# A decoder kernel on one core: the first normalisation moved ahead of the weights, and the first decay chain moved from VectorE to GpSimd

## The reference

```python
def _layernorm(x, axis=-1, eps=1e-05):
    m = jnp.mean(x, axis=axis, keepdims=True)
    v = jnp.var(x, axis=axis, keepdims=True)
    return (x - m) / jnp.sqrt(v + eps)

# _L0_attn, for the normalised x, two heads h of 128 features, chunks of 64 tokens
rk = x.reshape(Bs, Ts, H, d);  rk = rk / max(norm(rk), 1e-12)
beta = sigmoid(einsum('btd,hd->bth', x, W_beta))
log_decay = -exp(A_log) * softplus(einsum('btd,hd->bth', x, W_alpha) + dt_bias)
cum = cumsum(log_decay, -1)                       # within a chunk
L_mask = tril(exp(tril(cum[:, None] - cum[None, :])))
```

## Time and profile before

| what | value |
|---|---|
| median of 3 runs | 5632.31 us (5630.9 to 5637.03) |
| the profiled execution | 5640.22 us |
| its span, first to last instruction | 5637.7 us |
| PE, DVE, POOL, ACT busy | 4736.9, 4265.8, 3826.9, 2325.5 us |
| end of the piece in front of the loop | about 330.8 us into the span |
| mean granted TensorE clock | 0.95 |

### The profile page before, as it was taken

The page is one execution under the profiler, slowest core; times in us unless marked ns, Lnnn a source line. Parts: engine busy times, 40 slices in busy tenths (PEclk is TensorE's granted clock), DMA queues, the critical chain, the costliest instruction groups (busy, mean ns, idle before and its releaser), DMA issues.

```text
span 5637.7 us, 105981 instructions
## 1 busy us (share of the span) xinstructions
PE 4736.9 (84%) x28362; PEld 3112.3 (55%) x28362; DVE 4265.8 (76%) x11558; ACT 2325.5 (41%) x4480; POOL 3826.9 (68%) x10625
## 2 busy tenths in 40 slices
PE   1069898888889889888988988898898889889888
PEld 0045655656566465655646565565656556565655
DVE  5868777777777778777777878777787877778777
ACT  0034344444334444444444444444443444444344
POOL 1158676785867678586767858676785867768585
PEclk7589999999999999999999999999999999999999
DMA  3000000000000000000000000000000000000000
GB/s 85 8 12 1 28 1 13 16 9 20 1 24 5 11 18 9 20 1 24 5 9 20 9 20 1 24 5 9 20 5 24 1 24 5 9 20 1 20 1 16
DMA packets 61879, 78.07 MB, mean 14 GB/s; under 512 B 11168, under 2 KB 53808, under 8 KB 61232
## 3 DMA queue, kind: packets, MB, share of 16 engines
q1 hardware_dynamic: 52784, 62.42, 3.4%
q10 hardware_dynamic: 8448, 8.39, 0.4%
HBM read 45.04 MB, written 8.46 MB: 9 GB/s over the span
## 4 chain that ended last, share of the span: by engine, by line
PE 58%; DVE 23%; issue 8%; ACT 8%; POOL 1%; SPq 1%; DMA 1%; DVEq 0%; ACTq 0%; POOLq 0%
PE bank L1171 8%; PE bank L1090 6%; PE bank L1204 5%; PE bank L1076 5%; PE bank L1102 4%; PE bank L1000 3%; PE bank L1124 3%; PE bank L1007 3%; PE bank L1189 2%; PE bank L1111 2%; DVE arena L2004 2%; PE bank L1082 2%; ACT arena L763 2%; ACT arena L750 1%; PE bank L1132 1%
## 5 line engine op out<-in xcount | busy, mean ns | idle before, releaser
L746 ACT ACTIVATE arena<-bank 128x512 f32<-128x512 f32 x768 | 454.4, 592 | 386.9 <-PE bank L1090 386.9
L1775 DVE TENSOR_REDUCE smax<-bank 128x4 f32<-128x512 f32 x768 | 525.5, 684 | 114.6 <-PE bank L1082 66.1
L1779 DVE TENSOR_TENSOR arena<-bank,smax 128x512 f32<-128x512 f32 x768 | 531.2, 692 | 26.4
L1090 PE MATMUL bank<-ident,arena 128*128 128x128 f32 x3072 | 489.4, 282 | 46.9 <-ACT arena L737 29.2
L1171 PE MATMUL bank<-w,arena 128*128 128x512 f32 x1024 | 482.2, 601 | 14.0 <-DVE arena L1727 14.0
L1102 PE MATMUL bank<-arena 128*32 128x128 f32 x6144 | 329.1, 286 | 192.3 <-ACT arena L750 192.3
L1076 PE MATMUL bank<-arena 64*128 64x512 f32 x1536 | 436.4, 645 | 64.4 <-ACT arena L774 28.0
L1090 PEld LDWEIGHTS bank<-ident,arena 128*128 128x128 f32 x3072 | 348.7, 142 | 247.8 <-ACT arena L739 83.0
L1204 PE MATMUL bank<-w,arena 128*128 128x256 f32 x2048 | 454.1, 380 | 13.9 <-ACT arena L809 13.9
L737 ACT ACTIVATE arena<-arena,rstd 128x512 f32<-128x512 f32 x512 | 368.2, 719 | 203.4 <-DVE arena L1779 197.5
L1204 PEld LDWEIGHTS bank<-w,arena 128*128 128x128 f32 x2048 | 387.8, 190 | 90.3 <-issue 23.0
(11 more groups left out here) (428 smaller groups left out, 11948.0 us busy)
## 6 DMA issues: line engine op xcount, KB each, us to landing
arena<-in_x_dram SPq DMA_DIRECT2D x35, 512.0 KB, 3.5
xn_next<-arena SPq DMA_DIRECT2D x17, 512.0 KB, 2.9
arena<-cum_dram SPq DMA_DIRECT2D x17, 512.0 KB, 3.7
arena<-in_ctx_dram SPq DMA_DIRECT2D x16, 512.0 KB, 3.5
out_dram<-arena ACTq DMA_DIRECT2D x16, 512.0 KB, 3.1
xn<-xn_next SPq DMA_DIRECT2D x15, 512.0 KB, 2.9
w<-in_L_ffn_w_dram SPq DMA_DIRECT2D x8, 512.0 KB
w<-in_L_ffn_w_dram SPq DMA_DIRECT2D x1, 1024.0 KB
```

The lines of the kernel that those rows point to most:

```text
L746: act.activation(PT[:, v % 2], bank[3 + v % 2][:, :].rearrange("p (h q) -> p h q", h=QH), ACT.Copy).then_inc(S["pt"], 1)
L1090: ins = tr(bank[3 + v % 2][:, j * P:(j + 1) * P], Ssb[:, v % 4, j, :], ident[:, :])
L1775: dve.tensor_reduce(smax[:, u, :], sc, AX, ALU.max).then_inc(S["s_max"], 1)
L1779: dve.tensor_tensor(Ssb[:, u % 4], sc, smax[:, u, :].unsqueeze(2).broadcast_to([P, QH, P]), ALU.subtract).then_inc(S["s_sub"], 1)
```

## The change

The first `x_in` load and the two `W_alpha` loads are issued ahead of all other loads, and the latter get a semaphore of their own (`first_rows`). VectorE splits `W_alpha` and does the first norm before it waits for the weights; its set-up follows, then the second norm and the keys. GpSimd runs the first chain, behind its set-up and in front of `centered`. ScalarE's wait for weights and masks moves behind the first square-root seed. In the piece ahead of the loop both halves of a norm use the first set of scratch tiles.

```diff
         @block.sync
+            sp.dma_start(x_in[:, :, :], x_d[0]).then_inc(loaded_x, 16)
+            for h in range(DH):
+                sp.dma_start(dw[0][:, h, :], a["L0_attn_W_alpha"][h].partition_broadcast(P), ...).then_inc(first_rows, 16)
             for dst, src in loads:                 # without the two W_alpha loads
...
-            sp.dma_start(x_in[:, :, :], x_d[0]).then_inc(loaded_x, 16)
             sp.dma_start(xres[:, :, :], x_d[0]).then_inc(loaded_r, 16)
         @block.gpsimd
+            first = [0]
+            def first_link(operation, *operands, known=False, behind=0):
+                if first[0] > behind and not known:
+                    pool.wait_ge(first_step, first[0] - behind)
+                operation(*operands).then_inc(first_step, 1)
+                first[0] += 1
+            pool.wait_ge(set_dve, 2)
+            pool.wait_ge(moved_now, 16)
+            for j in range(SLICES):
+                chain_products(pool, first_link, xn0[:, :, :], j)
+                chain_links(pool, first_link, j, 0, 16)
+            chain_end(pool, first_link)
+            pool.wait_ge(first_step, first[0])
+            pool.tensor_tensor(au[:, :], acc_a[:, :, 0], acc_a[:, :, 1], ALU.add).then_inc(au_ready, 1)
             centered(0, 0)
             first_squares(0, 0)
             decay_table(0, 0)
         @block.scalar
-            act.wait_ge(w_loaded, 16 * len(loads))
-            act.wait_ge(set_pool, SET_POOL)
...
-            for n in range(2):
-                variance_seed(n)
+            variance_seed(0)
+            act.wait_ge(w_loaded, 16 * len(loads))
+            act.wait_ge(set_pool, SET_POOL)
+            variance_seed(1)
         @block.tensor
-            pe.wait_ge(set_dve, 1)
+            pe.wait_ge(set_dve, SET_RGB)           # 4
         @block.vector
-            (wait for weights and masks, set-up of the weights)
...
-                quo, quo_p, quo_e, quo_h, quo_l = quotients[m]
+                quo, quo_p, quo_e, quo_h, quo_l = quotients[0 if run["first"] else m]
...
+            dve.wait_ge(first_rows, 32)
+            link(dve.tensor_scalar(dw[1]..., dw[0]..., HIGH_BITS, None, ALU.bitwise_and))
+            link(dve.tensor_tensor(dw[2][:, :, :], dw[0], dw[1], ALU.subtract))
-            for n in range(2):
+            def first_norm(n):
                 run["n"] = n
                 exact_sums()
...
+            first_norm(0)
+            dve.wait_ge(w_loaded, 16 * len(loads))
+            dve.wait_ge(set_pool, SET_POOL)
+            (the set-up of the weights, without the split of W_alpha)
+            first_norm(1)
             dve.wait_ge(moved_now, 16)
             key_limit(0, 0)
             key_rows(0, 0, xn0)
-            for j in range(SLICES):
-                chain_products(dve, chain_link, xn0[:, :, :], j)
-                chain_links(dve, chain_link, j, 0, 16)
-            chain_end(dve, chain_link)
-            dve.wait_ge(first_step, first[0])
-            tt(au[:, :], acc_a[:, :, 0], acc_a[:, :, 1], ADD).then_inc(au_ready, 1)
             beta_rows(0, 0)
```

More of the change, by code:

```diff
@@ L1321, in _ @@
-            link(dve.tensor_copy(bcol[:, :], bank[2][:, 6 * HD:6 * HD + 6]))
-            link(dve.tensor_tensor(halfbias[:, :], halfmask[:, :], bcol[:, 3:4].broadcast_to([P, QH]), ALU.mult))
-            dve.wait_ge(set_pe, 2)
-            link(dve.tensor_copy(rsum[:, :, :].rearrange("p a e -> p (a e)"), bank[3][:, 0:2 * E0]))
-            assert n_set[0] == SET_ROUTER, n_set[0]
-            for c in range(C):
-                link(dve.scalar_tensor_tensor(out=rgb[:, c, 0, :], in0=rsum[:, 0, :], scalar=-1.0 / D, in1=rgb[:, c, 0, :], op0=ALU.mult, op1=ALU.add))
@@ L1340, in _ @@
             r = lambda n: row[:, n, :]
-            run = {"n": 0, "at": 0, "before": 0, "ref": 0, "decay": 0, "d": 0}
+            run = {"first": True, "n": 0, "at": 0, "before": 0, "ref": 0, "decay": 0, "d": 0}
             def step(ins):
@@ L1446, in exact_last @@
             def exact_last(m):
-                quo = quotients[m][0]
+                quo = quotients[0 if run["first"] else m][0]
                 xr = x_in[:, 2 * m:2 * m + 2, :]
@@ L1626, in _ @@
             key_rows(0, 0, xn0)
-            first = [0]
-            def chain_link(operation, *operands, known=False, behind=0):
-                if first[0] > behind and not known:
-                    dve.wait_ge(first_step, first[0] - behind)
-                operation(*operands).then_inc(first_step, 1)
-                first[0] += 1
-            for j in range(SLICES):
-                chain_products(dve, chain_link, xn0[:, :, :], j)
-                chain_links(dve, chain_link, j, 0, 16)
-            chain_end(dve, chain_link)
-            dve.wait_ge(first_step, first[0])
-            tt(au[:, :], acc_a[:, :, 0], acc_a[:, :, 1], ADD).then_inc(au_ready, 1)
             beta_rows(0, 0)
@@ L1654, in _ @@
             with nc.Fori(0, NIT, engines=[dve.engine], hint_back_edge=True) as it:
+                run["first"] = False
                 run["at"], run["n"], run["d"], run["before"], run["ref"], run["decay"] = it, 2, 1, REF_BEFORE, 0, 0
@@ L2025 @@
 SET_POOL = 62
-SET_ROUTER = 14
-SET_DVE = 28
+SET_RGB = 4
+SET_ROUTER = 15
+SET_DVE = 29
 KM_BEFORE = (0, 2, 4)
```

55 lines of the change are left out of this document (29 added, 26 removed).

## The result

The changed kernel takes 5661.64 us (median of 7 runs, 5651.77 to 5680.56), the kernel before in the same comparison 5635.71: the ratio is 1.0051, interval 1.0033 to 1.0069. The prediction said 5626.9, no measurable difference, and 5616 to 5637 as the range; the time lies above it. The profiled execution took 5680.56 us with a span of 5678.7 and a mean granted TensorE clock of 0.941, where the one of before had 5637.7 and 0.950. It is the longest of its seven runs, so its trace shows the loss larger than the medians do.

A forecast was written before the change was run, and what follows sets the result against it. VectorE was taken to be alone on the path ahead of the loop, the 16 passes left alone. Earlier chain start -98.0, chain on GpSimd +88.6, decay collisions +4.0: -5.4 us, so 5632.3 - 5.4 = 5626.9, range 5616 to 5637.

The forecast's parts named there:

- Start of the first norm: VectorE ahead of the loop: loads land at 7.0 us, `W_alpha` split takes 1.2, so the norm starts at 8.2.
- The first norm: VectorE ahead of the loop: 38.8 us alone plus 2.5 for GpSimd's set-up running beside it, ending at 49.5.
- The copy: SyncE's copy between first norm and chain: 3.0 us, ends 2.9 and 6.0, so the chain starts at 52.5.
- The chain: First chain on GpSimd ahead of the loop: 221.1 us plus 10.5 for collisions with VectorE, against 143 on VectorE.
- First decay step: VectorE behind the chain: starts at 284.2 us instead of 293.57, 9.4 us earlier.
- Collisions in the decays: GpSimd's `centered` and `first_squares` hold up VectorE's decay steps ahead of the loop: +4.0 us, ends 0 and 7.
- Behind the chain: Decays to loop entry: collisions cost 4.0 us, shrinking 9.4 to 5.4; exchange, table, first level and TensorE clock stay alike.
- Collisions nearly free: Ahead of the loop: set-up costs the norm nothing, chain pays 3 instead of 10.5; gain 15.4 us, 5616.9; chance 0.14.
- Exclusion: Second norm beside the chain: GpSimd stands still while VectorE is busy; result 18.7 us slower, 5651; chance 0.05.
- rival 2: VectorE and GpSimd exclude each other in the second norm: chain pays 34.6 us instead of 10.5; 5651; chance 0.05.
- Factor two: Chain ahead of the loop takes 286 us on GpSimd, 54 more than forecast, giving 5681; chance 0.01.
- 98 us won, 93 given back by the engine change: Ahead of the loop: chain starts 98.0 us earlier; moving it to GpSimd costs 88.6, decay collisions 4.0; together -5.4 us.

The follow-up runs named there:

- the fill: Four scratch matmuls per pass in TensorE's wait behind `residual_features(3)`: changed kernel 5662.48 us (1.0034), kernel before 5635.75 (0.9985), chain on VectorE 5593.23 (0.9909).
- 595 fillers: Changed kernel plus 595 one-element memsets on VectorE while it waits for GpSimd's chain: 5659.85 us, 1.0016 of before.
- 592 fillers: Changed kernel plus 592 one-element memsets on VectorE while it waits for GpSimd's chain: 5711.04 us (1.0117) in the first set, 5685.70 (1.0070) in the fifth.

## Why the prediction was wrong

**Ahead of the loop it was right**, to 1.5 us at every step and to 0.5 us at the entry. *Start of the first norm* 8.2: 8.88. *The first norm* 38.8 + 2.5 ending at 49.5: it ran 42.06 and ended at 50.9. *The copy* 3.0: 3.1. *The chain* 221.1 + 10.5 = 231.6 from 52.5: it took 229.6 from 54.04 to the first decay step, a group 2.40 us against 2.41, with the large strokes (1.18 and 1.30) where the second norm's centring and squares ran. *First decay step* 284.2: 283.68. *Collisions in the decays* +4.0: the two strokes came as said, 1.75 and 1.70, and loop entry moved by 5.93 us against the forecast 5.4.

**The step that failed is in its first paragraph and in "Behind the chain": "leave the 16 passes, over 94% of the span, alone", with "so the loop starts alike".** The change to the loop's cost was put at nothing for the one reason that TensorE does as little ahead of it as before. The loop did not cost the same: 46.9 us more in the traces, and some 32 in the medians (25.9 us lost and 5.9 won ahead of the loop). The prediction's own signs of being wrong (2.41 us for a group, a chain that starts after 60, a short gap before the decays) all looked in front of the loop, and all came out as forecast.

What the runs showed in its place is two things. Taking the chain out of VectorE's program moves VectorE's gaps in every pass: with the fill in both kernels, 592 idle instructions put back on VectorE took 23.2 us off. And each pass has a stretch at 181 to 184 us in which TensorE waits for VectorE twice; a few tenths of a microsecond more in the first wait go with a fall to 1.2 GHz for up to 17 us. Filling the second wait removed this fall from every pass, but it did not make the changed kernel faster: its loss then stood behind 278 us of the pass. The rows of the fall were to be had: two of the 16 passes of before, of 339.2 and 335.2 us, already had it.

**What tips it** is shown in part. VectorE has gaps of 0.2 to 0.3 us at places fixed by how far its loop stands in its program; the change took some 600 instructions out of the piece in front of VectorE's loop, so the gaps moved, in the changed kernel into the decay steps. Shifting the loop by three instructions moved a gap and 25.9 us. Open is why the kernel with GpSimd's chain stays above before even with 595 fillers, what made before itself take 5688 us in one set, and how to remove the fall at 317 us; filling the wait ahead of it and splitting the thin matmuls both failed. That the gaps come from the loading of instructions is what the traces suggest and no run tested.

**The rivals.** Collisions nearly free: no, 10.5 charged and 8.5 found. Exclusion: no; GpSimd ran 594 operations beside 140 of VectorE and lost 8.5 us where rival 2 had 34.6. By the Trainium skill (SBUF — State Buffer, "SBUF: two separate sides"), the port pair that the two engines share is held for a whole instruction. The strokes of 1.18 and 1.30 us, beside two VectorE operations of 1.23 us each, agree with that for long operations, while the whole chain lost 8.5 us beside 53.67 us of VectorE work. Factor two: the chain took 229.6 us against 143.0, a factor of 1.6. By the Trainium skill (GPSIMD Engine Reference, 4.1 Engine selection), elementwise work with two inputs is about twice as slow on GpSimd; this trace has less.

**The reason behind the sum was right and not followed to its end.** "98 us won, 93 given back by the engine change" already says that the two halves should be tried apart. With the chain left on VectorE the loop is entered 44.6 us earlier, and with the first fill the kernel takes 5593.23 and 5590.76 us in two sets: 0.9909 (0.9893 to 0.9924) and 0.9916 (0.9902 to 0.9930) of before. It is faster than both kernels.

## What to carry to other kernels

A move that relieves one engine ahead of the path is worth splitting: here the early load and norm won 44.6 us and the slower engine's chain gave 38.6 back. A loop whose code is untouched is not thereby unchanged: look in the trace of before for the few passes that are longer, and find the wait that stands in front of their lower clock. Filling it is cheap and made the kernel with the chain on VectorE steadier, but check by the medians that it is what the change lost: here it was not all. When instructions leave the piece in front of an engine's loop, put as many idle ones in their place once, to tell the effect of the place from that of the work. When a change is worth under 1%, repeat the unchanged kernel in more than one set of runs; here it moved by 0.9% between two sets on one chip.

## What the runs showed of the hardware that I had not expected

- Passes can repeat one bad pattern: twelve passes of 337.9 us in a row in one trace, 331.1 us three times running in another, with the falls at the same microsecond of each.
- The same program has executions in which GpSimd's 10513 loop operations are busy 13 us longer, 1.3 ns for each. The kernel before shows both (3782.74 and 3796.14), with `au` about 1 us later in each pass in the second. The changed kernel was near the second in all three of its traces. The kernel with 592 fillers, with more falls than any other, is near the first (3781.24), so it is not what makes the falls. Whether it is chance is open.
- VectorE's gap of 0.2 to 0.3 us between two dependent steps at fixed places of the program, 0.8 to 1.3 us ahead of a packet of the instruction queue, which three more instructions in front of the loop move.
